# The second mixture's tiles with wider buffers, all high parts on VectorE and one register operation for each weight half

## The reference

```python
scores = sigmoid(x @ gate_w.T)                      # 16 experts, 4 of them chosen for each token
tidx, tw = _route(x, gate_w, gate_bias)             # groups of 4 experts, the best 2 groups, then the top 4
combine = zeros((n, E)).at[arange(n)[:, None], tidx].add(tw)
g = einsum('nh,eih->nei', x, w1)                    # 256 -> 192
u = einsum('nh,eih->nei', x, w3)                    # 256 -> 192
hact = silu(g) * u * combine[:, :, None]
y = einsum('nei,ehi->nh', hact, w2)                 # 192 -> 256
shared = (silu(x @ ws1.T) * (x @ ws3.T)) @ ws2.T    # one expert that every token passes
```

## Time and profile before

| | us |
|---|---|
| median of three runs | 1565.94 (1562.79 to 1566.61) |
| the profiled execution's own time | 1566.47 |
| its span, first to last instruction | 1564.6 |

### The profile page before, as it was taken

One profiled execution on the slowest core, in us unless ns is written; L12 is line 12 of the kernel. 1 busy time (PEld: TensorE's weight loads), 2 busy tenths in 40 slices (PEclk: granted clock), 3 DMA queues, 4 the chain that ended last, 5 costly groups with the idle time before them and its releaser, 6 DMA issues. The chain is left out here.

```text
span 1564.6 us, 40990 instructions
## 1 busy us (share of the span) xinstructions
PE 1200.6 (77%) x13450; PEld 872.8 (56%) x13450; DVE 1102.2 (70%) x2985; ACT 781.1 (50%) x2076; POOL 447.2 (29%) x480
## 2 busy tenths in 40 slices
PE   4899999997667542999999974876895065999950
PEld 2688888885334331998888853432464033666630
DVE  5799999996799988795555536433657886666646
ACT  6688888885423231784444430521455115665530
POOL 0555555550200000002333320020020017477740
PEclk9999999998888865999999995877996559999985
DMA  2433333321000039201111117579203502233328
GB/s 93 100 80 81 81 81 78 78 70 59 1 0 1 0 101 359 91 2 33 51 51 49 49 32 241 176 226 349 80 1 108 233 20 75 62 106 103 103 72 268
DMA packets 111807, 150.27 MB, mean 96 GB/s; under 512 B 13625, under 2 KB 96962, under 8 KB 111682
## 3 DMA queue, kind: packets, MB, share of 16 engines
q1 hardware_dynamic: 95730, 112.80, 23.1%
q0 software_dynamic: 11328, 30.95, 6.4%
q10 hardware_dynamic: 4624, 4.85, 1.0%
HBM read 126.80 MB, written 21.76 MB: 95 GB/s over the span
## 5 line engine op out<-in xcount | busy, mean ns | idle before, releaser
L1231 ACT ACTIVATE mixture_and_attentions_h<-ps,mixture_and_attentions_b 128x128 f32<-128x128 f32 x440 | 125.3, 373 | 126.5 <-PE ps L1183 125.2
L1183 PE MATMUL ps<-xture_and_attentions_m_w 128*128 128x128 f16 x1872 | 155.9, 219 | 1.7 <-DVE xture_and_attentions_m_w L1261 1.7
L1183 PEld LDWEIGHTS ps<-xture_and_attentions_m_w 128*128 x1872 | 129.1, 98 | 36.5 <-issue 2.6
L1505 POOL DMA_INDIRECT tage_second_mixture_rows<-n_rows,e_second_mixture_r_token x79 | 88.2, 1116 | 140.1 <-SPq L1336 116.3
L1269 DVE TENSOR_SCALAR ixture_and_attentions_hs<-mixture_and_attentions_h 128x512 f16<-128x512 f32 x110 | 47.2, 429 | 112.7 <-PE ps L1202 97.8
L1300 POOL DMA_INDIRECT ture_and_attentions_rows<-n_rows,e_and_attentions_r_token x39 | 38.7, 992 | 307.1 <-SPq L1138 208.8
L641 POOL TENSOR_TENSOR ads_and_recurrence_ctx_s<-ads_and_recurrence_ctx_c,ads_and_recurrence_ctx_s 128x512 f16<-128x512 f32 x64 | 74.2, 1160 | 177.4 <-ACT ads_and_recurrence_ctx_s L570 177.4
L590 ACT ACTIVATE ads_and_recurrence_probs<-ps,s_and_recurrence_neg_max 128x257 f32<-128x257 f32 x256 | 117.7, 480 | 1.1 <-DVE s_and_recurrence_neg_max L672 1.1
L1201 PE MATMUL ps<-xture_and_attentions_m_w,ixture_and_attentions_hs 128*128 x312 | 117.5, 379 | 0.2 <-DVE xture_and_attentions_m_w L1280 0.2
L1386 PE MATMUL ps<-stage_second_mixture_m_w,stage_second_mixture_x_s 128*128 x474 | 91.5, 330 | 2.0 <-issue 1.9
L1509 POOL DMA_INDIRECT y_rows<-stage_second_mixture_y,ge_second_mixture_r_dest x79 | 77.4, 980 | 41.9 <-DVE stage_second_mixture_y L1486 21.8
(11 more groups left out here) (391 smaller groups left out, 3376.8 us busy)
## 6 DMA issues: line engine op xcount, KB each, us to landing
ads_and_recurrence_ctx_t<-in_ctx_t SPq DMA_DIRECT2D x64, 257.0 KB, 2.7
e_and_attentions_b_ctx_t<-in_ctx_t SPq DMA_DIRECT2D x14, 1028.0 KB, 9.1
ure_and_attentions_b_ctx<-in_ctx SPq DMA_DIRECT2D x28, 512.0 KB, 8.2
xture_and_attentions_m_w<-in_m_w SPq DMA_DIRECT2D x2, 5632.0 KB, 37.4
ds_and_recurrence_mask_i<-in_mask SPq DMA_DIRECT2D x256, 32.1 KB, 1.7
stage_second_mixture_c_y<-y_rows SPq DMA_DIRECT2D x16, 512.0 KB, 5.0
stage_second_mixture_m_w<-in_m_w SPq DMA_DIRECT2D x2, 3840.0 KB, 20.5
xture_and_attentions_m_w<-in_m_w SPq DMA_DIRECT2D x1, 5120.0 KB, 16.6
```

The source lines that it names most:

```text
L1183: last = pe.matmul(ps[:, UB + 2 * (u % 2) + f // PER, (f % PER) * P:(f % PER + 1) * P], slots.of(e, c, at, P), a[:, c, :], start=(n == 0), ...
L1231: last = act.activation(h32[n][:, at:at + P], ps[:, UB + 2 * (u % 2) + n, at:at + P], ACT.Silu, scale=1 / (WS * NS), bias=b1[:, bass.ds(e ...
L1505: pool.indirect_dma_start(rows[s % R][:, :], None, k.n_rows, bass.IndirectOffsetOnAxis(ap=r.token[:, s:s + 1], axis=0)).then_inc(k.t_rows[ ...
```

## The change

Four things change, all in `second_tiles`. `high` runs on VectorE for all 95 tiles, and ScalarE's `high` is gone. There are eight `y` buffers in place of four, so `result` of tile `s` waits for scatter `s - 8`. There are 48 row buffers in place of 32, and a semaphore counts batches of six gathers in place of four; with `R = 48` GpSimd's list starts with 44 gathers, and before scatter `s` it has issued `44 + 35 * (s + 1) // 67`. Last, `weight` puts the choice between the high and the low half into the constant that `Slots.of` adds to the register, instead of into the slice that is taken afterwards.

```diff
-    R = 32
+    BATCH = 6
+    R, Y = 8 * BATCH, 8
...
-        y = [k.sb(f"y{b}", [P, D], ctx=ctx) for b in range(4)]
+        y = [k.sb(f"y{b}", [P, D], ctx=ctx) for b in range(Y)]
...
             def weight(u, x, lo, n):
-                both = slots.of(expert(u), 0, 2 * lo, 2 * n).rearrange("p (b x n) -> p b x n", x=2, n=P)
-                return both[:, :, x, :]
+                both = slots.of(expert(u), 0, 2 * lo + x * P, 2 * n).rearrange("p (b x n) -> p b x n", x=2, n=P)
+                return both[:, :, 0, :]
...
             def turn(u):
                 s = u - NT
-                pe.wait_ge(k.t_rows[s // 4 % 8].sem, k.t_rows[s // 4 % 8].at(loads(s // 4)))
+                pe.wait_ge(k.t_rows[s // BATCH % 8].sem, k.t_rows[s // BATCH % 8].at(loads(s // BATCH)))
...
-            def high(u):
-                act.wait_ge(k.t_gated.sem, k.t_gated.at(u + 1))
-                act.wait_ge(k.t_flip.sem, k.t_flip.at(u - 2))
-                act.activation(hs[u % 3][:, 0:I1], h32[u % 3][:, :], ACT.Copy).then_inc(k.t_high.sem, 1)
-
...
             for u in range(3):
                 silu(u)
-                high(u)
...
-                if u + 3 < NT:
-                    high(u + 3)
...
-                if s >= 4:
-                    dve.wait_ge(k.t_stored[s % 4].sem, k.t_stored[s % 4].at(s // 4))
-                dve.tensor_scalar(y[s % 4][:, :], out, 1 / (WS * HS), None, ALU.mult).then_inc(k.t_ycopied.sem, 1)
+                if s >= Y:
+                    dve.wait_ge(k.t_stored[s % Y].sem, k.t_stored[s % Y].at(s // Y))
+                dve.tensor_scalar(y[s % Y][:, :], out, 1 / (WS * HS), None, ALU.mult).then_inc(k.t_ycopied.sem, 1)
 
             for u in range(3):
                 multiply(u)
+                high(u)
                 low(u)
...
-                    if u + 3 >= NT:
-                        high(u + 3)
+                    high(u + 3)
                     low(u + 3)
```

More of the change, by code:

```diff
@@ L1344, in loads @@
         def loads(batch):
-            return sum(min(4, mix.tiles - 4 * n) for n in range(batch % 8, batch + 1, 8))
+            return sum(min(BATCH, mix.tiles - BATCH * n) for n in range(batch % 8, batch + 1, 8))
         def source(u):
@@ L1504, in gather @@
                 pool.wait_ge(k.t_trans.sem, k.t_trans.at(s - R + 1))
-                pool.indirect_dma_start(rows[s % R][:, :], None, k.n_rows, bass.IndirectOffsetOnAxis(ap=r.token[:, s:s + 1], axis=0)).then_inc(k.t_rows[s // 4 % 8].sem, 16)
+                pool.indirect_dma_start(rows[s % R][:, :], None, k.n_rows, bass.IndirectOffsetOnAxis(ap=r.token[:, s:s + 1], axis=0)).then_inc(k.t_rows[s // BATCH % 8].sem, 16)
             def scatter(s):
                 pool.wait_ge(k.t_ycopied.sem, k.t_ycopied.at(NT + s + 1))
-                pool.indirect_dma_start(k.y_rows, bass.IndirectOffsetOnAxis(ap=r.dest[:, s:s + 1], axis=0), y[s % 4][:, :], None).then_inc(k.t_stored[s % 4].sem, 16)
+                pool.indirect_dma_start(k.y_rows, bass.IndirectOffsetOnAxis(ap=r.dest[:, s:s + 1], axis=0), y[s % Y][:, :], None).then_inc(k.t_stored[s % Y].sem, 16)
             gathered = 0
@@ L1516, in _ @@
                 scatter(s)
-            for b in range(4):
-                pool.wait_ge(k.t_stored[b].sem, k.t_stored[b].at((mix.tiles + 3 - b) // 4))
+            for b in range(Y):
+                pool.wait_ge(k.t_stored[b].sem, k.t_stored[b].at((mix.tiles + Y - 1 - b) // Y))
     for s in (k.t_up, k.t_act, k.t_gated, k.t_high, k.t_low, k.t_flip, k.t_hcopied, k.t_down, k.t_ycopied):
@@ L1522, in second_tiles @@
         s.base += mix.tiles
-    for b in range(4):
-        k.t_stored[b].base += (mix.tiles + 3 - b) // 4
+    for b in range(Y):
+        k.t_stored[b].base += (mix.tiles + Y - 1 - b) // Y
     for s in range(mix.tiles):
-        k.t_rows[s // 4 % 8].base += 1
+        k.t_rows[s // BATCH % 8].base += 1
     slots.finish()
@@ L2249, in build @@
         k.m_cwt = k.count("m_cwt")
-        k.t_trans = k.count("t_trans", 32)
+        k.t_trans = k.count("t_trans", 48)
         k.t_xcopied = k.count("t_xcopied", 2)
@@ L2302, in build @@
         k.t_rows = [k.count(f"t_rows{p}", unit=16) for p in range(8)]
-        k.t_stored = [k.count(f"t_stored{p}", unit=16) for p in range(4)]
+        k.t_stored = [k.count(f"t_stored{p}", unit=16) for p in range(8)]
         k.x_loaded = [k.count(f"x_loaded{g}", unit=16) for g in range(G)]
```

## The result

The changed kernel took 1545.31 us (median of four runs, 1542.96 to 1547.98), the kernel before 1564.37 (1562.49 to 1566.61) beside it. The ratio is 0.9879, 95% interval 0.9862 to 0.9896: 19.1 us less, where 18.0 were forecast (1548.0 us, or 0.9885). The profiled execution took 1542.96 us with a span of 1541.1, from the first instruction to the last.

The account below looks back on a forecast made before the run. GpSimd's list was taken to bound the block: tile 72 at 1472.6, plus 12.4 and 9.9 us, puts the last scatter at 1494.9 instead of 1512.9. That is 18.0 us less: 1548.0 us, range 1543 to 1558.

Parts of the forecast that it names:

- The place of the bound: Routed tiles: GpSimd's full list of gathers and scatters, 1.285 us each, sets when the last scatter is issued.
- T: GpSimd: time when the 44 early gathers end and scatters can begin, forecast 1343, bounds 1337.5 and 1352.1.
- tile 72: TensorE's tile that needs gather 77, the last of its batch: can't start before T + 129.6 = 1472.6.
- The period: Shared tiles: low splits 2.80 us apart instead of 3.72, set by VectorE; eleven periods save 10.1 us.
- The hold per split: Shared tiles: each low weight split on VectorE delays a gather by 0.30 us, 12 of them 3.6.
- The added copies: Rival: `high` copies on VectorE hold up gathers, up to 5 us, T = 1348, time 1553; chance 0.08.
- TensorE's pace: Routed tiles: 2.07 us a tile through shorter register operations, from 2.14; pays 0.4 us in the last six tiles.
- waits for batches at tiles 60 and 66: Sign of error: the prediction is wrong if TensorE waits for a batch of gathers before tile 72.
- The eight result buffers: VectorE, routed tiles: remove 24.4 us of waits for scatters, the same time seen from the other side; add nothing.
- Gathers held through the rest of every split: Rival, shared tiles: 12 x 1.22 us whatever the period, T = 1352.1, time 1557; chance 0.18 together with shared tiles not shortened.
- Shared tiles not shortened: Rival: another ring holds 3.7 us, first result stays at 1343.8, time 1557; chance 0.18 together with gathers held through.
- Gathers that take the gain away: Rival: 44 gathers delay the first scatter until the gain is gone, from T = 1361 on; chance 0.08, half of it slower.

Follow-up runs that it names:

- c4_buffers_alone: The kernel before with only 48 row buffers, batches of six and eight result buffers: 1560.12 us, ratio 0.9968 to the kernel before.
- d4_two_ops_again: The changed kernel with the weight half taken by a slice again, the longer register operation: 1545.85 us, ratio 0.9880 to the kernel before.
- d3_high_back_again: The changed kernel with `high` of the 16 shared tiles back on ScalarE: 1555.73 us, ratio 0.9934 to the kernel before.
- c3_one_op_alone: The kernel before with only `weight` changed, the half put into the address constant: 1563.31 us, ratio 0.9992 to the kernel before.
- d2_batches_of_four: The changed kernel with twelve batches of four gathers (still 48 row buffers) and four result buffers: 1538.67 us, ratio 0.9828 to the kernel before.
- the first four experiments: The changed kernel with one part undone each (`high`, `weight`, result buffers, 28 gathers ahead), on a chip where the kernel before took 1644.55 us: 1632.25 to 1641.00 us.
- c2_high_alone: The kernel before with only `high` moved to VectorE: 1552.05 us, ratio 0.9913 to the kernel before.
- e3_four_results: The changed kernel with four result buffers instead of eight, on a chip where the kernel before took 1644.55 us: 1632.25 us, ratio 0.9914.

## Why the prediction was right

**The place of the bound.** Right for the changed kernel: the end follows GpSimd's list. Last scatter minus T is 152.0 us (151.9 forecast), 152.8 in its second profile, 153.3 with `high` back, 145.4 with denser gathers and 146.6 with batches of four. It isn't so in every kernel: with TensorE at 2.13 us a tile it is 157.7 (`c4_buffers_alone`) and 155.1 (`d4_two_ops_again`), as GpSimd waits for results there. The changed kernel is free of this by its faster register operations, a part for which the prediction booked 0.4 us. By its parts: tile 72 at T + 130.2 (129.6), the last `turn` 12.8 later (12.4), the last scatter 9.0 after it (9.9).

**The period.** 2.75 us against 2.80. VectorE's own order sets it, and `d3_high_back_again` shows that the handover was the cause. First result: 13.3 us sooner, counted from the first gather, 10.8 forecast. Eleven periods gave 10.7 (10.1 forecast), the first split 1.1 (0.6), and from the last split to the first result it is 1.5 us less (11.5 before, 10.0 after), which the prediction had left unchanged. Those 1.5 are no part of the sum, as the gathers end later than that anyway.

**T.** 58.2 us after the first gather, 60.5 forecast (1343 less 1282.50). The hold per split was 0.25, 0.30 forecast; the 1.9 us that were added for unsettled first splits were not needed in this profile. In the second one a gather beside the first split took 2.08, and T is 59.4. With the 3.3 us by which the block began sooner this makes 1489.43 out of 1494.9. That early start is no part of the forecast. The two profiled executions differ by 23.5 us and the medians by 19.1, so that the forecast of 18.0 comes so near to the medians is in part luck: the block itself gained 20.2 us in one profile and 18.2 in the other.

**The added copies.** Early gathers took 0.95 us (a few up to 1.02) where no split held them, as before; the rival that priced them at 5 us is out, since T lies below the forecast and not above it. The Trainium skill ("SBUF — State Buffer", section "Who interferes with whom") lets the first to issue hold the shared ports for its whole instruction. For the weight split the trace agrees in one direction: the gather that met it was held until it ended. In the other it doesn't: the split at 1292.32 issued 0.14 us behind a gather and still took 1.48, no more than the splits of the kernel before, which had no gather ahead of them (1.49). The copies show a hold too, but mostly of the copy and a small one (a scatter and a copy of the changed kernel):

```profile
1474.36 0.97 POOL L1502 DMA_INDIRECT y_rows<-stage_second_mixture_y,ge_second_mixture_r_dest  x1 [1.13 <-DVE stage_second_mixture_y L1479]
...
1474.93 0.46 DVE L1463 CAST stage_second_mixture_hs<-stage_second_mixture_h 128x192 f16<-128x192 f32 x1
```

A copy that starts 0.23 to 0.42 us before the end of a gather or scatter ends 0.06 to 0.08 us behind it; one that starts 0.47 us or more before that end takes its 0.26. In the changed kernel this befalls 13 of the 95 copies, with under 2 us in all. A gather that started 0.06 us behind a copy took 1.06, not 0.99 (1380.08). So the trace has a hold here, but not over the whole instruction, and at a fraction of the price that the rival gave it.

**TensorE's pace: the term that was mis-sized.** "I take 2.07" of a range of 2.00 to 2.14; it was 1.91. I kept 0.30 to 0.55 us for each load of expert numbers, which "stays", and thought most of the 94 ns hidden beside matmuls. In fact the five shorter operations of a tile removed the whole excess, and the step at the loads with it (`c3_one_op_alone` and `d4_two_ops_again` differ in `weight` alone from their neighbours, and show 1.91 against 2.17). By 1.91 TensorE would start tile 72 near 1327.1 + 68 x 1.91 - 2.8 = 1454, and it waited from 1456 to 1467.60. The error cost nothing, as the sum went by the later of the two, the gather. That was luck in part, since by the slower pace of `d4_two_ops_again` the two do meet. The text called the two "close", and they were 11 us apart. It also listed waits for batches at tiles 60 and 66 as a sign of error. TensorE did wait at tile 66, 0.78 us (the row at 1443.94; 0.53 in the second profile), with the period, T and the end as forecast: a TensorE that runs early meets such a wait. That sign was badly chosen.

**The eight result buffers.** "They remove the 24.4 us of waits on VectorE, which is the same time as above" and add nothing. Right in the whole; 5.5 us of waits are left. That they aren't needed at all while GpSimd is full, the text didn't say; `d2_batches_of_four` shows it with batches of four.

**The other rivals.** Gathers held through the rest of every split, T at 69.6 after the first gather: that is the state of `c4_buffers_alone` (68.5) and `d3_high_back_again` (68.6), where the period stays 3.73. It is what the long period makes of the same hold. Shared tiles not shortened: out by the 2.75. Gathers that take the gain away (T = 1361): out; even in `c4_buffers_alone`, with T 6.5 us later than before, the kernel won 4.9 us.

**What stays open.** Whether 44 gathers ahead beat 28 within the changed kernel was tried by itself only on the chip of the first four experiments. The nearest answer elsewhere is the 6.2 us between `c2_high_alone` and `d4_two_ops_again`, where all the buffers change together. Moving `high` and changing the register operation without the buffers wasn't run. Batches of four with the denser spread weren't tried together; by the count of 114 instructions they should give no more than either. The stretch of 11.4 to 11.5 us between the last scatter and the first read of `combine` stayed in every kernel outside the first four, and wasn't taken apart.

## What to carry to other kernels

When an engine's list of equally priced instructions is full, count what stands in it behind the first event that you can move: the end is that event plus a constant as long as the list stays full, and faster neighbours only change who waits (TensorE's 0.2 us a tile became a wait, VectorE's in the kernel before, its own in the changed one). Look again after each part, though: a shorter list can empty, and then the same 0.2 us a tile counts (4.4 us between `c4_buffers_alone` and `d3_high_back_again`). A helper engine with idle time is not free: a short copy that is handed over and comes back behind other work can hold the busy engine up by more than it takes itself. And a batch that shares a semaphore makes its first user wait for its last member, so place the last member by that user.

## What the runs showed of the hardware

**Short register operations set TensorE's pace.** The edit to `weight` touches five operations of a tile on TensorE's sequencer: three at L1387, which go from 51, some 102 and some 111 ns to 46, 32 and 32, the one at L1404 from 100 to 32, and the one at L1406 from 94 to 32. That is some 0.28 us less a tile, an estimate from these rows, and the tile takes 1.91 us instead of 2.13. So most of it shows in the pace. Which matmul each delays I didn't follow.

**Gathers beside which everything else stands still.** On the chip of the first four experiments, while GpSimd issued gathers, the other engines hardly ran. Two windows of `e3_four_results` (length, then busy us and instructions of TensorE, its loads, VectorE, ScalarE and GpSimd, then the granted clock, the DMA share and GB/s), one with gathers and one after them, and three instructions out of the first:

```profile
1300.00:1335.00 35.00, 4.17 (x18) 2.39 (x19) 3.93 (x10) 3.54 (x6) 26.65 (x28) 0.51 0.40 102
1345.00:1360.00 15.00, 11.23 (x87) 7.21 (x85) 14.62 (x35) 11.43 (x18) 0.00 (x0) 0.99 0.01 2
```

```profile
1325.37 0.33 ACT L1434 ACTIVATE stage_second_mixture_h<-ps 128x192 f32<-128x192 f32 x1 [17.35 <-issue]
...
1332.68 0.95 POOL L1498 DMA_INDIRECT tage_second_mixture_rows<-n_rows,e_second_mixture_r_token  x1 [0.30 <-issue]
1333.78 0.49 ACT L1439 ACTIVATE stage_second_mixture_h_t<-ps 128x384 f16<-128x384 f16 x1 [8.07 <-remote]
...
1334.32 0.39 PE L1402 MATMUL ps<-stage_second_mixture_m_w,stage_second_mixture_h_t 128*128 128x256 f16 x1 [23.91 <-issue]
```

TensorE was busy 4.17 of 35 us, and stood 23.91 us before one matmul with no releaser in the profile, while the gathers kept their 0.95 us. When they stopped, VectorE was busy 14.62 of 15 us. The runs elsewhere show nothing of this with the same instructions. The cause wasn't found, and as the kernels ran there only once, in one group, the chip and the time of the runs can't be told apart. One more row may bear on it: the queues that bring instructions moved one packet from 1300 to 1335 us in `e3_four_results`, and five in the same 35 us of the changed kernel. That can be the cause, or just follow from engines that stand still.
